# One core, a decoder block: the attention's prefix mask as a contraction row, and its row shifts transposed in one product

## The reference, cut to what matters

```python
sg = jnp.einsum('bhcqd,bhkd->bhcqk', qc, kg) * scale      # 16 prefix keys
st = jnp.einsum('bhcqd,bhckd->bhcqk', qc, kt) * scale     # window keys
mg = jnp.arange(P)[None, None, :] <= q_pos[:, :, None]
mt = (diff >= 0) & (diff < W) & (kt_pos[:, None, :] >= P)
scores = jnp.concatenate([jnp.where(mg[None, None], sg, neg), jnp.where(mt[None, None], st, neg)], axis=-1)
attn = jax.nn.softmax(scores, axis=-1)
```

## Time and profile before

| | |
|---|---|
| time, median of 3 | 1231.37 us (1230.73 to 1235.14) |
| span of the profiled execution | 1231.3 us |
| PE busy | 1156.3 us, 94% of it |
| DVE, ACT, POOL busy | 762.9 (62%), 529.5 (43%), 506.5 (41%) us |
| mean granted TensorE clock | 0.991 |

### The profile page before, as it was taken

One profiled execution on the slowest core, in us unless ns is written; L12 is line 12 of the kernel. 1 busy time (PEld: TensorE's weight loads), 2 busy tenths in 40 slices (PEclk: granted clock), 3 DMA queues, 4 the chain that ended last, 5 costly groups with the idle time before them and its releaser, 6 DMA issues. The chain is left out here.

```text
span 1231.3 us, 27541 instructions
## 1 busy us (share of the span) xinstructions
PE 1156.3 (94%) x8847; PEld 785.6 (64%) x8848; DVE 762.9 (62%) x2136; ACT 529.5 (43%) x1123; POOL 506.5 (41%) x718
## 2 busy tenths in 40 slices
PE   8999999999999999999898999999999999999995
PEld 3546455464554645546454466666667999999995
DVE  4555667757767577665635557666674565556653
ACT  5445454545454544545452255544433333333330
POOL 3334325244152442433421122444353556655664
PEclk9999999999999999999999999999999999999998
DMA  7284654644737346374273123434313111111110
GB/s 217 74 222 123 176 148 121 177 117 133 186 99 200 85 136 183 89 194 112 78 199 85 50 78 103 142 134 162 110 41 98 51 42 51 50 55 51 52 44 7
DMA packets 142637, 137.83 MB, mean 112 GB/s; under 512 B 29545, under 2 KB 135919, under 8 KB 142449
## 3 DMA queue, kind: packets, MB, share of 16 engines
q1 hardware_dynamic: 136976, 124.23, 36.2%
q0 software_dynamic: 5280, 12.66, 3.0%
q10 hardware_dynamic: 320, 0.16, 0.1%
HBM read 49.41 MB, written 50.83 MB: 81 GB/s over the span
## 5 line engine op out<-in xcount | busy, mean ns | idle before, releaser
L972 ACT ACTIVATE probs<-ps_b 128x512 f32<-128x512 f32 (+2 forms) x352 | 174.5, 538 | 91.8 <-PE ps_b L1439 36.5
L593 POOL TENSOR_SCALAR_AFFINE_SELECT probs<-probs 128x512 f32<-128x512 f32 x128 | 82.1, 641 | 267.8 <-ACT probs L972 264.5
L2840 PE MATMUL ps_c<-keep_w,e_hT 128*128 x624 | 141.0, 379 | 0.0
L2840 PEld LDWEIGHTS ps_c<-keep_w,e_hT 128*128 128x128 f32 x624 | 115.7, 190 | 14.1
L714 DVE CUSTOM_DVE_ANT_0 ps_a<-ps_a,mask_qk 128x256 f32<-128x256 f32 x224 | 88.9, 450 | 18.8 <-PE ps_a L1263 18.7
L708 DVE TENSOR_REDUCE top<-ps_a 128x2 f32<-128x512 f32 (+1 forms) x112 | 74.1, 683 | 30.1 <-PE ps_a L1263 29.3
L1263 PE MATMUL ps_a<-k_rows,q_rows 96*128 96x256 bf16 (+1 forms) x512 | 84.9, 262 | 4.6 <-DVE top L714 2.7
L1819 ACT ACTIVATE e_w_now<-keep_w 128x1024 f32 x78 | 78.1, 1049 | 22.0 <-issue 12.1
L2800 ACT ACTIVATE e_yT<-ps_d 128x256 f32<-128x256 f32 x39 | 14.9, 383 | 167.8 <-PE ps_d L2819 167.8
L2829 PE MATMUL ps_a<-e_yT,e_w_now 128*128 128x128 f32 x640 | 76.1, 278 | 0.0
L1294 PE MATMUL ps_b<-q_rows,k_rows 98*128 98x256 bf16 (+1 forms) x512 | 75.7, 261 | 0.2
(11 more groups left out here) (248 smaller groups left out, 2470.4 us busy)
## 6 DMA issues: line engine op xcount, KB each, us to landing
sorted_rows<-filler SPq DMA_DIRECT2D x8, 4290.0 KB, 18.3
q_rows<-parts SPq DMA_DIRECT2D x96, 128.0 KB, 2.4
k_rows<-parts SPq DMA_DIRECT2D x96, 128.0 KB, 2.4
q_rows<-q_parts SPq DMA_DIRECT2D x96, 128.0 KB, 2.4
keep_w<-in_e_w SPq DMA_DIRECT2D x16, 512.0 KB, 4.4
keep_w<-in_e_w SPq DMA_DIRECT2D x8, 1024.0 KB, 8.1
e_row<-sorted_rows SPq DMA_DIRECT2D x39, 130.0 KB, 2.1
x_in<-in_x SPq DMA_DIRECT2D x8, 512.0 KB, 4.4
```

Source lines behind the costliest of these rows:

```text
L593: nc.gpsimd.affine_select(own, own, [[0, TILES], [1, P]], ALU.is_ge, keep_zero, base=0, channel_multiplier=-1).then_inc(probs_cut.sem, 1)
L972: nc.scalar.activation(probs[:, user % 2, lo:lo + width], ps_exp[:, f % 2, 0:width], ACT.Exp).then_inc(exp_done.sem, 1)
L2840: mm = nc.tensor.matmul(ps_out[:, s, 0:D], hT[:, s, f, :], w2[:, bass.ds(e * KF * D + f * D, D)], start=(f == 0), stop=(f == KF - 1))
```

## The change

Two edits, both in the attention.

1. `mask_prefix` and its product go. `q_rows` and `k_rows` get a 99th row: in `k_rows`, for keys 0 to 31, it is 0 for the 16 prefix keys and the mask value behind them; in `q_rows` it is ones. Both are loaded once by DMA, so there are 16 constants instead of 15. The four products of the prefix contract 99 rows and begin the accumulation themselves; all other products name 98 rows.
2. `shift` is laid out as [128 queries, 2 parts, 16 heads, 4 tiles], so that the whole is a 128 x 128 tile, turned by one product. For half the heads the other places stay zero. DVE's two instructions write runs of one value at a distance of 8 bytes. ACT copies 128 x 128 instead of 32 x 512. The DMAs read `shiftT` with one row for each head and tile, so that a run is 128 queries, 256 bytes, four times as many of them.

```diff
-                const(mask_prefix[:, :], t["c_mask_prefix"])
+                const(k_rows[SHIFT_ROWS:PREFIX_ROWS, :, 0:32],
+                      t["c_mask_qk"][PREFIX - 1:PREFIX, 1:2, P:P + 32].broadcast_to([1, HEADS, 32]))
+                const(q_rows[SHIFT_ROWS:PREFIX_ROWS, :, :].rearrange("o h (a b) -> o (h a) b", b=P // 2),
+                      t["c_before"][0:1, P // 2:P].unsqueeze(1).broadcast_to([1, HEADS * S // (P // 2), P // 2]))
...
                     for part in range(2):
                         sp.dma_start(q2_rows[SPLIT_ROWS + part:SPLIT_ROWS + part + 1, :, :],
-                                     shiftT2[part * HEADS:(part + 1) * HEADS, :]).then_inc(shift2_stacked.sem, 16)
+                                     shiftT2[part * HEADS * TILES:(part + 1) * HEADS * TILES, :]).then_inc(shift2_stacked.sem, 16)
...
-                    nc.vector.tensor_scalar(out[:, :, 0:heads], tops, -1.0, None, ALU.mult).then_inc(hi.sem, 1)
+                    high, low = (out[:, part, 0:heads, :].rearrange("p h c -> p c h") for part in range(2))
+                    nc.vector.tensor_scalar(high, tops, -1.0, None, ALU.mult).then_inc(hi.sem, 1)
...
-                    nc.scalar.activation(out[:, :], ps.bitcast(BF16)[0:2 * HEADS, 0:S], ACT.Copy).then_inc(sig.sem, 1)
+                    nc.scalar.activation(out[:, :], ps.bitcast(BF16)[:, 0:P], ACT.Copy).then_inc(sig.sem, 1)
...
-                    for c in range(TILES):
-                        mm = nc.tensor.transpose(ps.bitcast(BF16)[0:2 * HEADS, c * P:(c + 1) * P], src[:, c, :], ident[:, :])
-                    mm.then_inc(work_full.sem, 1)
+                    nc.tensor.transpose(ps.bitcast(BF16)[:, 0:P], src[:, :, :, :].rearrange("p t h c -> p (t h c)"), ident[:, :]
+                                        ).then_inc(work_full.sem, 1)
...
                     ps = exp_claim(n, f)
-                    nc.tensor.matmul(ps[:, 0:256], ident[:, :], mask_prefix[:, :], start=True, stop=False,
-                                     skip_group_check=True)
                     for j, h in enumerate(group_heads(g)):
                         mm = nc.tensor.matmul(ps[32 * j:32 * j + 32, 0:256], k_rows[:, h, 0:32], q_rows[:, h, 256:512],
-                                              start=False, stop=True, skip_group_check=True)
+                                              start=True, stop=True, skip_group_check=True)
...
-N_CONST = 6 + 5 + 4
+N_CONST = 7 + 5 + 4
```

More of the change, by code:

```diff
@@ L36 @@
 SHIFT_ROWS = SPLIT_ROWS + 2
+PREFIX_ROWS = SHIFT_ROWS + 1
 PAIRED = ((0, 0), (0, 1), (0, 2), (1, 0), (1, 1), (2, 0))
@@ L162, in attention_program @@
         mask_first = sb("mask_first", [P, P], BF16)
-        mask_prefix = sb("mask_prefix", [P, 256], BF16)
         ctx_rows = sb("ctx_rows", [P, D])
@@ L191, in attention_program @@
         rest = sb("rest", [P, 4, S])
-        q_rows = sb("q_rows", [SHIFT_ROWS, HEADS, S], BF16)
-        k_rows = sb("k_rows", [SHIFT_ROWS, HEADS, S], BF16)
+        q_rows = sb("q_rows", [PREFIX_ROWS, HEADS, S], BF16)
+        k_rows = sb("k_rows", [PREFIX_ROWS, HEADS, S], BF16)
         v_ones = sb("v_ones", [P, TILES, HEADS, 32])
@@ L200, in attention_program @@
         top2 = sb("top2", [P, TILES, HEADS])
-        shift = [sb(f"shift{h}", [P, TILES, 2 * HEADS], BF16) for h in range(2)]
-        shiftT = [sb(f"shiftT{h}", [2 * HEADS, S], BF16) for h in range(2)]
-        shift2 = sb("shift2", [P, TILES, 2 * HEADS], BF16)
-        shiftT2 = sb("shiftT2", [2 * HEADS, S], BF16)
+        shift = [sb(f"shift{h}", [P, 2, HEADS, TILES], BF16) for h in range(2)]
+        shiftT = [sb(f"shiftT{h}", [P, P], BF16) for h in range(2)]
+        shift2 = sb("shift2", [P, 2, HEADS, TILES], BF16)
+        shiftT2 = sb("shiftT2", [P, P], BF16)
         probs = sb("probs", [P, 2, GROUP_COLS])
@@ L475, in stack_shift @@
                         sp.dma_start(q_rows[SPLIT_ROWS + part:SPLIT_ROWS + part + 1, top_half(0), :],
-                                     shiftT[0][part * HALF:(part + 1) * HALF, :]).then_inc(shift_stacked[0].sem, 16)
+                                     shiftT[0][part * HEADS * TILES:part * HEADS * TILES + HALF * TILES, :]).then_inc(shift_stacked[0].sem, 16)
                 def copy_prefix(n):
@@ L659, in _ @@
                 for tile in (shift[0], shift[1], shift2):
-                    nc.gpsimd.memset(tile[:, :, :], 0.0).then_inc(consts_set.sem, 1)
+                    nc.gpsimd.memset(tile[:, :, :, :], 0.0).then_inc(consts_set.sem, 1)
                 pool.wait_ge(consts_loaded.sem, 16 * N_CONST)
@@ L748, in shift_parts @@
                 def shift_parts(n, tops, out, heads, hi, his, ready):
-                    nc.vector.tensor_scalar(out[:, :, 0:heads], tops, -1.0, None, ALU.mult).then_inc(hi.sem, 1)
+                    high, low = (out[:, part, 0:heads, :].rearrange("p h c -> p c h") for part in range(2))
+                    nc.vector.tensor_scalar(high, tops, -1.0, None, ALU.mult).then_inc(hi.sem, 1)
                     dve.wait_ge(hi.sem, hi.count(n, his))
-                    nc.vector.scalar_tensor_tensor(out[:, :, heads:2 * heads], tops, -1.0, out[:, :, 0:heads],
+                    nc.vector.scalar_tensor_tensor(low, tops, -1.0, high,
                                                    ALU.mult, ALU.subtract).then_inc(ready.sem, 1)
@@ L1113, in iteration @@
                         act.dma_start(q_rows[SPLIT_ROWS + part:SPLIT_ROWS + part + 1, top_half(1), :],
-                                      shiftT[1][part * HALF:(part + 1) * HALF, :]).then_inc(shift_stacked[1].sem, 16)
+                                      shiftT[1][part * HEADS * TILES:part * HEADS * TILES + HALF * TILES, :]).then_inc(shift_stacked[1].sem, 16)
                     if front:
@@ L1293, in window_shifted @@
                                 q0, q1 = kt * P, min(kt + 2, TILES) * P
-                                mm = nc.tensor.matmul(ps[:, 256 * i:256 * i + q1 - q0], k_rows[:, h, kt * P:(kt + 1) * P],
-                                                      q_rows[:, h, q0:q1], start=(kt == 2), stop=True, skip_group_check=True)
+                                mm = nc.tensor.matmul(ps[:, 256 * i:256 * i + q1 - q0], k_rows[0:SHIFT_ROWS, h, kt * P:(kt + 1) * P],
+                                                      q_rows[0:SHIFT_ROWS, h, q0:q1], start=(kt == 2), stop=True, skip_group_check=True)
                             mm.then_inc(exp_full.sem, 1)
```

## The result

| | before | changed |
|---|---|---|
| median | 1233.26 us (1230.73 to 1235.83, 4 runs) | 1225.05 us (1222.23 to 1226.33, 4 runs) |
| span of the profiled execution | 1231.3 us | 1224.6 us |
| mean granted clock of it | 0.991 | 0.991 |

The ratio is 0.9925, with a 95% interval of 0.9905 to 0.9945. The forecast was 1222.2, with a range of 1218.5 to 1229: the time lies within it, 2.9 us above the forecast. From the 1231.37 that the sum started from, the change brought 6.3 us where 9.1 were forecast. By the medians of this table it brought 8.2, by a second comparison further down only 4.9. That has to be explained as well as the parts of the sum.

The account below looks back on a forecast made before the run. PE's list was taken to bound the attention, with short ACT and DVE hand-offs between its stretches. Gains of 6.7 us (six samples), 0.8 (prologue, sample 0) and 1.6 (sample 7, closing) sum to 9.1: 1231.3 to 1222.2, range 1218.5 to 1229.

Parts of the forecast that it names:

- first rival: Hand-offs with ACT or DVE absorb half the gain: 0.66 us a steady sample, 1226.3 us in all; chance 0.25.
- shiftT2: Its single transpose, after a wait for DVE: between PE's 0.27 and ACT's 0.44 us gained, taken as 0.36 a sample.
- Group 2: Mask product removed from this group's prefix fill, where PE waits for ACT ahead of it: 0.21 us gained a steady sample.
- Groups 0 and 3: Mask removed from prefix fills behind f32 products, where the step to narrow products costs 0.20: 0.07 us gained in each.
- Group 1 and shiftB: Group 1's mask gives 0, swallowed by a 0.20 wait for DVE's maximum; shiftB's single transpose gives 0.12 us.
- shiftA: Its single transpose, with a shorter copy on busy ACT: between 0.27 and 0.43 us gained, taken as 0.30 a steady sample.
- The step from full to narrow: PE's change from full-width to 32-column products ahead of the prefix products: 0.10 us that stays when the mask goes.
- Prologue and sample 0: Two shiftA at 0.27, one mask at 0.2, one at 0.07; the others lie ahead of DVE waits: 0.8 us.
- The DMAs: Shift rows in 32 or 64 runs of 256 bytes land as fast as before: no change, between -0.2 and +0.5 us.
- the rival of the short runs: Shift rows land late as runs multiply: 6 us of waits at twice the landing time; chance 0.07 including other delays.
- my step for the start of the kernel: Two small constants replace one, delaying SP's next load 0 to 0.2 us and POOL 0.4 to 0.9: counted 0, at most 0.3 lost.
- The clock: Stretches at the lower granted clock: one more costs about 1.7 us, one fewer gives as much; in the range, no case.

Follow-up runs that it names:

- second comparison: The changed kernel run once more without any edit, beside the kernel before: 1226.04 us, ratio 0.9965; its profile is the second trace.
- The run with dense writes: Changed kernel with row maxima stored heads first, tiles last, so DVE's two shift instructions read and write runs without gaps: 1224.18 us, ratio 0.9946.
- the long copy: Changed kernel with ACT's copy of the turned shift writing each column four times (128 x 512), to last as long as before: 1227.23 us, ratio 0.9968.
- the narrow masks: Changed kernel's new shift, with the mask back as four products of 32 array columns instead of one of full width: 1225.56 us, ratio 0.9963.
- The shift alone: Kernel before with only one transpose for each shift, the mask product kept: 1225.98 us, ratio 0.9967.
- the mask alone: Kernel before with only the prefix mask as a 99th row, shifts still turned in four products: 1228.27 us, ratio 0.9979.
- the later turn: Changed kernel with gapless DVE shift writes, and shiftT2's transpose and copy moved behind the next two fills and their exponentials: 1220.62 us, ratio 0.9908.

## Why the prediction was right, point by point

**The total.** The sum said 9.1 us, and the change is worth 6 to 7: it was too high by 2 to 3 us, less than the range allowed for. Up to the end of the attention the first trace shows 11.3, of which about 2.8 (1.3 and 1.5) belong to the two stretches of low clock that before had and the changed kernel had not; 8.5 are left. That is more than 6 to 7: of the difference 1.2 us are lost behind the attention, and neither they nor the rest are traced. The terms missed on both sides:

| stretch (PE's starts) | forecast | first trace |
|---|---|---|
| start to the prefix of group 0 in sample 1 (108.37) | 0.8 | 2.3 |
| to the same place in sample 2 (189.36) | 1.0 | 1.1 (2.4 less 1.3 of clock) |
| four steady samples (505.16) | 4.5 | 3.4 |
| to the end of the attention (682.82) | 2.8 | 1.7 (3.2 less 1.5 of clock) |

So it was partly luck: two errors cancelled. Nor does the time tell the forecast from its first rival. The prediction drew the line between the two at 1225.2; the first measurement, 1225.05, is just under it and the second, 1226.04, just above. The period tells more: a steady sample gains 0.85, and that is nearer to the 0.66 of rival 1 than to the 1.13 of the sum.

**shiftT2 was taken too high** (0.36, measured 0.17). The term counted 0.27 on PE and a share of ACT's 0.44. It left out that the next full-width product starts 0.11 behind the turn and not 0.055, and it set DVE's strided writes to 0 where they cost 0.12 of waiting. The run with dense writes gives the 0.12 back, which is the proof for this part. For the 0.055 I have the rows and no cause.

**Group 2 was taken too high** (0.21, measured 0.08). The mask's 0.21 did go there. I had looked only at what releases PE ahead of the fill, not at the second product behind it, which takes its bank from DVE: 0.14 came back as a wait. This is rival 1 in one place. Of the 0.47 that rival 1 takes off a sample, 0.28 came.

**Groups 0 and 3 were taken too low** (0.07 each, measured 0.11 and 0.10). I worked from halves of f32 durations; the mask's plain 0.11 was the better number. The dearer step behind f32 products, 0.20, was a misreading of the earlier trace rows: of the 0.20 by which those four f32 products take longer, 0.11 lies ahead of their second product and only 0.09 at the end, ahead of the narrow one. In group 3 the four products of 256 columns take 0.92 up to the full-width mask before and 1.02 up to the narrow products now:

```profile
248.32 0.27 PE L1301 MATMUL ps_b<-mask_prefix,ident 128*128 128x256 bf16 x1
```

```profile
242.08 1.08 PE L1392 MATMUL ps_d<-w_v,ctxT 128*128 128x256 f32 x4
243.10 0.29 PE L1305 MATMUL ps_b<-q_rows,k_rows 99*32 99x256 bf16 x4
```

So the step is 0.10 behind f32 products as well. Group 1 and shiftB came out as the prediction put them (0; 0.13 for 0.12). shiftA gave 0.26, for 0.30 and just under the 0.27 that was to be the least, and all of it through ACT: with the long copy the wait for ACT is back.

**The step from full to narrow** stayed when the mask went, as the prediction said: the narrow masks show it ahead of whichever narrow product comes first. By the Trainium skill ("TensorEngine Tiling (Array Packing)", Key Properties) it is the change of tiling mode that drains TensorE; the run with the narrow mask agrees, with 0.09 to 0.10 us.

**Prologue and sample 0 were taken too low** (0.8, measured 2.3). I had written off what lies ahead of waits for DVE. One of these waits, 0.39 at 71.54 before, vanished itself, with 0.56 and 0.16 gained behind it. The shift alone shows it, the mask alone does not. On ACT the copy of shiftB and the issue of its two DMAs stand ahead of the split of the next queries (`parts`), on which DVE waits. The two issues, before and with the shift alone:

```profile
66.88 1.95 ACTq L1113 DMA_DIRECT2D q_rows<-shiftT  x2
```

```profile
65.89 1.25 ACTq L1115 DMA_DIRECT2D q_rows<-shiftT  x2
```

The copy takes 0.27 instead of 0.57, and the two issues take 0.70 less. The prediction did not count what an issue takes on ACT at all. Of the 2.3, 0.23 stand ahead of everything that the change touches on PE (11.03 instead of 11.26 at the first f32 product) and were 0.05 in the second trace. There the DMAs behind the long fill took 1.0 us back.

**The DMAs.** No change at 256 bytes where before gives a number: 2.2 us for shiftT2 against 2.1. shiftA's rows take 1.9 and shiftB's, issued by ACT, 2.4, against the expected 1.9 to 2.3; the trace of before has no landing for these two. Nothing waits for the rows in the loop. But the rival of the short runs deserved a closer bound, and my step for the start of the kernel named SP's issues and POOL and missed the DMAs that are issued behind the long fill of sample 0.

**The clock.** It was put at one stretch more or fewer, 1.7 us each. It was the largest disturbance of a single comparison: two stretches fewer in the attention, two more behind it.

## What to carry to other kernels

Price a removed instruction by the distance of starts, then follow both of its neighbours to their next hand-off, the one behind as closely as the one ahead: most of what was missed here, in both directions, lay one product further on. When two traces run the same list, take the difference of partner starts and read where it steps; it told gains of 0.1 us where whole executions spread over 6. And when the profile shows an idle piece ahead of the very instruction that is being made cheaper, try to move it as well: the later turn gave 0.68 us a sample, more than the new shift itself.

## What the runs showed that I had not expected

- 128 and 256 runs of a DMA of 16 KB are not alike: 2.5 and 3.9 us to land, against 2.1 for 16 runs and 2.2 for 64.
- Four products of 32 columns of the array and 256 columns of data, for different columns of the array, take 0.12 us up to the next narrow product, about as long as one of full width takes (0.11).
- Two small DVE writes of bf16 at a distance of 8 bytes (64 values per partition) took 0.24 and 0.30 us instead of 0.20 and 0.22.
- Right behind a DMA of 4290 KB the next issue on SP took 10.27 us instead of 0.64, and 8 KB issued some 10 us behind it took 8 to 10 us to land.
- The first of ACT's DMA issues in the prologue took 0.62 us with 32 runs of 256 bytes, where it took 1.28 with 8 runs of 1024. The cause is open.
- Open: whether the short runs make it worse when the DMA engines are that busy. The two traces with the old runs show no wait in sample 0, three of those with 256-byte runs and the fill in its old place show none either, and the issues stand at different times. Open too is what decides where the clock falls: in the second trace of the changed kernel it stayed up at two of the three places where it fell in the first.
